# QKV products of a decoder's self-attention as a 2x2 block product in seven products, with heads in pairs

## The chip, the cores and the metric

The kernel runs on one core of a Trainium2 chip. Its engines are TensorE (PE, matmuls; PEld is its weight load), VectorE (DVE), ScalarE (ACT), GpSimd (POOL) and SyncE (SP, which issues most transfers). The metric is the device time of one launch in microseconds; lower is better.

## The reference

A decoder of two layers over 16 sequences of 112 tokens, 1024 wide, in float32. The change touches the self-attention of the second layer, where "sequence" runs over the first axis of `x`, of length 16 (`sbh` with s = 16, b = 112), so attention is causal over 16 positions, for 112 independent columns:

```python
def _L1_attn_ref(tokens, weight_qkv, weight_proj):
    NUM_HEADS, NUM_KV_HEADS, HEAD_DIM = (32, 8, 128)
    Q_PER_GROUP = NUM_HEADS // NUM_KV_HEADS
    qkv = jnp.einsum('sbh,ph->sbp', tokens, weight_qkv)
    qkv = qkv.reshape(S, B, NUM_KV_HEADS, Q_PER_GROUP + 2, HEAD_DIM)
    ...
    scores = jnp.einsum('bhsd,bhtd->bhst', q, k) * scale
    scores = jnp.where(causal, scores, jnp.finfo(scores.dtype).min)
    attn = jax.nn.softmax(scores, axis=-1)
    out = jnp.einsum('bhst,bhtd->bhsd', attn, v)
    return jnp.einsum('sbe,he->sbh', out, weight_proj)

x = _layernorm(x + _L1_attn_ref(x, L1_attn_weight_qkv, L1_attn_weight_proj), axis=-1)
```

So 1792 tokens are multiplied with 6144 x 1024 weights (8 groups of one key, one value and four query units of 128 features), 32 heads attend, and 4096 x 1024 weights project back.

## The kernel before

Three stages run one after the other: `token_stage` for layer 0, `self_attention` for layer 1, `token_stage` for the rest of layer 1. Only `self_attention` differs (and where the experts' weights lie in a shared buffer).

The 1792 tokens are handled in two halves of 896 (`TH`; seven chunks `c` of 128 tokens, `NC`). Each half runs over the eight key/value heads; one half and one head is a group `G`, so there are 16 groups. Every product of float32 data is three products of rounded parts, hi x hi, hi x lo, lo x hi (`split_passes`, type float32r). The tokens, transposed, lie in `x_hi` and `x_lo` for the half at hand; the rows of the second half are prepared one per group in groups 0 to 6 (`early`), stored, and reloaded at group 8 (`NKV`).

A group on TensorE: units K, V, Q0 to Q3. A unit is `product` (L1445) twice, over 480 and 416 columns (K, V) or 480 and 360 (Q: the first of the 16 positions needs no query, its columns lie last), each with 8 k-tiles x 3 passes accumulated in one PSUM bank. Inside the units come the transposes of the values (`turn_values`, L1474), the scores of a head (`scores`, L1466, one burst of 28 small matmuls, 56 records) and, after the next group's K, the weighing (`weigh`, L1487: four matmuls of 32 rows for each chunk) and the projection (`project`, L1504: for each chunk and each half of the output 4 heads x 3 passes of 512 columns). Projections go through a ring of three PSUM banks; each key of the table `slot` says which.

GpSimd walks down a table `splits`: for each 128 x 1024 piece of weights it waits for the load and for a free buffer, casts it to the hi part (L1386) and subtracts to get the lo part (L1388). `w_hi`/`w_lo` hold two units, `p_hi`/`p_lo` the four heads' projection weights. SP loads pieces in the same order through two buffers `raw`. ScalarE copies products from PSUM to `qT`, `kT`, `vT` (L1589), takes exponentials (L1598) and casts the weighed values (L1612). VectorE does the softmax (L1711 to L1728), the low parts of the weighed values (L1733) and adds the projection to `acc` (L1745). At a half's end the group's last scores, weighing and projection follow with no next group to hide them (`ends_half`).

Every order is written out by hand; nothing is scheduled by a planner.

## Time and profile before

| | us |
|---|---|
| median of 3 runs | 3245.8 (3244.6 to 3246.4) |
| span of the profiled execution | 3248.6 |
| TensorE busy | 3091.6 (95%) |
| VectorE busy | 1803.7 (56%) |
| ScalarE busy | 1341.0 (41%) |
| GpSimd busy | 873.5 (27%) |
| self-attention, first product to last projection | 830.2 to about 2546 |

Busy times are those of one profiled execution, counted from its first instruction. Matmuls are pipelined, so the record of one is longer than the distance to the next; where the pace matters, one reads the starts. The granted clock of TensorE is 1.00 at 2.4 GHz and 0.50 at 1.2 GHz. Lines named L... are those of the kernel before; in the section on the order of the changed kernel they are those of the changed one.

### The profile page before, as it was taken

Reading aid. Unit: us, or ns where it says so; the run is one execution under the profiler, and the core shown is the slowest. Engines: PE = TensorE matmul, PEld = TensorE weight load, DVE = VectorE, ACT = ScalarE, POOL = GpSimd, SP = SyncE. Lnnn points to the kernel's source line nnn. Section 1 sums busy time; section 2 is a strip of 40 time slices with the busy share of each in tenths; the row PEclk is TensorE's granted clock in tenths of the full one; section 3 lists DMA queues with packets and bytes.
Section 4 is the critical chain, followed back from the end, with each engine's and each line's share of the span. In section 5 each row is a group of like instructions: output and inputs, shape, how many; then the busy total and the mean of one; then the engine's idle time right before and its main releaser. Section 6 shows DMA issues by size and latency. Waiting matters only on the chain. (4 is left out here: it accounts for less than half of the span.)

```text
span 3248.6 us, 67042 instructions
## 1 busy us (share of the span) xinstructions
PE 3091.6 (95%) x25912; PEld 2575.3 (79%) x25912; DVE 1803.7 (56%) x4632; ACT 1341.0 (41%) x3692; POOL 873.5 (27%) x751
## 2 busy tenths in 40 slices
PE   5999999996999999999989999999999699999997
PEld 3888888874788888888878888888887578888886
DVE  6788888885424332544253323333243488888885
ACT  2777877774211111111111111111111487777774
POOL 3222222211423432243225332443233011111110
PEclk8999999996899999999999999999999899999999
DMA  9777777752212311231144111221124656555551
GB/s 282 187 188 188 195 199 189 188 144 91 72 52 79 92 58 53 72 92 59 52 163 143 53 59 60 84 76 55 53 72 156 161 148 151 151 151 151 151 148 44
DMA packets 226622, 386.73 MB, mean 119 GB/s; under 512 B 55953, under 2 KB 177137, under 8 KB 225794
## 3 DMA queue, kind: packets, MB, share of 16 engines
q1 hardware_dynamic: 222848, 380.25, 42.2%
q8 instruction: 207, 3.39, 0.5%
q10 hardware_dynamic: 3458, 2.20, 0.2%
q14 instruction: 109, 0.89, 0.1%
HBM read 291.46 MB, written 90.91 MB: 118 GB/s over the span
## 5 line engine op out<-in xcount | busy, mean ns | idle before, releaser
L749 ACT ACTIVATE L_probs<-L_masked,L_least 112x375 f32<-112x375 f32 x1024 | 627.8, 615 | 80.0 <-DVE L_least L878 75.7
L878 DVE CUSTOM_DVE_ANT_0 L_masked<-L_scores,L_nmask 112x375 f32<-112x375 f32 x1024 | 552.6, 544 | 174.3 <-PE L_scores L482 137.0
L1445 PE MATMUL sa_banks<-both_hi,sa_w_hi 128*128 128x480 f32 (+2 forms) x1536 | 560.2, 365 | 2.0 <-DVE both_lo L1704 2.0
L1445 PE MATMUL sa_banks<-both_lo,sa_w_hi 128*128 128x480 f32 (+2 forms) x1536 | 550.6, 358 | 0.0
L1445 PE MATMUL sa_banks<-both_hi,sa_w_lo 128*128 128x480 f32 (+2 forms) x1536 | 549.7, 358 | 0.0
L487 PEld LDWEIGHTS L_turned<-ident_sb,L_probs 112*125 112x125 f32 x3072 | 457.1, 189 | 108.2 <-issue 48.2
L487 PE MATMUL L_turned<-ident_sb,L_probs 112*125 112x112 f32 x3072 | 526.7, 280 | 7.6 <-ACT L_probsT L744 3.9
L482 PE MATMUL L_scores<-L_krep,L_qrep 128*112 128x376 f32 x1024 | 418.1, 409 | 7.8 <-DMA L_qrep<-query_parts 6.0
L744 ACT COPY L_probsT<-L_turned 125x336 f32<-125x336 f32 x768 | 337.3, 439 | 177.8 <-PE L_turned L487 170.6
L1745 DVE TENSOR_TENSOR sa_acc<-sa_acc,sa_banks 128x512 f32<-128x512 f32 x224 | 154.1, 688 | 416.9 <-PE sa_banks L1504 416.9
L1504 PE MATMUL sa_banks<-sa_p_hi,sa_o_hi 128*128 128x512 f32 x896 | 365.5, 408 | 0.0
L1504 PE MATMUL sa_banks<-sa_p_lo,sa_o_hi 128*128 128x512 f32 x896 | 355.3, 397 | 0.0
L1504 PE MATMUL sa_banks<-sa_p_hi,sa_o_lo 128*128 128x512 f32 x896 | 355.0, 396 | 0.0
L1445 PEld LDWEIGHTS sa_banks<-both_hi,sa_w_hi 128*128 128x128 f32 x1536 | 288.9, 188 | 34.7 <-issue 6.8
L1711 DVE SCALAR_TENSOR_TENSOR sa_sm<-sa_banks,sa_causal 128x224 f32<-128x224 f32 x64 | 25.1, 392 | 511.0 <-PE sa_banks L1466 511.0
L1445 PEld LDWEIGHTS sa_banks<-both_hi,sa_w_lo 128*128 128x128 f32 x1536 | 288.9, 188 | 23.5
L1445 PEld LDWEIGHTS sa_banks<-both_lo,sa_w_hi 128*128 128x128 f32 x1536 | 289.4, 188 | 21.7
L1612 ACT CAST sa_o_hi<-sa_banks 128x512 fp32r<-128x512 f32 x112 | 66.0, 589 | 508.4 <-PE sa_banks L1487 506.7
L384 POOL TENSOR_TENSOR L_attn<-L_attn,L_xcur 112x512 f32<-112x512 f32 x64 | 82.6, 1291 | 588.5 <-DVEq L891 588.5
L1388 POOL TENSOR_TENSOR sa_w_lo<-sa_raw,sa_w_hi 128x1024 fp32r<-128x1024 f32 x96 | 230.0, 2396 | 14.4 <-issue 1.0
L1386 POOL CAST sa_p_hi<-sa_raw 128x1024 fp32r<-128x1024 f32 x64 | 66.6, 1041 | 565.6 <-PE sa_banks L1504 554.4
L1504 PEld LDWEIGHTS sa_banks<-sa_p_hi,sa_o_hi 128*128 128x128 f32 x896 | 169.0, 189 | 47.9 <-issue 0.4
(289 smaller groups left out, 5055.3 us busy)
## 6 DMA issues: line engine op xcount, KB each, us to landing
L_qrep<-query_parts SPq DMA_DIRECT2D x256, 224.0 KB, 6.2
sa_raw<-in_wqkvU_dram SPq DMA_DIRECT2D x96, 512.0 KB, 3.5
L_krep<-ctx_parts SPq DMA_DIRECT2D x256, 188.0 KB, 4.2
sa_raw<-in_wprojU_dram SPq DMA_DIRECT2D x64, 512.0 KB, 3.5
query_parts<-L_qT_hi SPq DMA_DIRECT2D x64, 224.0 KB, 8.4
query_parts<-L_qT_lo SPq DMA_DIRECT2D x64, 224.0 KB, 9.3
L_xcur<-x SPq DMA_DIRECT2D x32, 448.0 KB, 5.1
L_val<-in_ctx_dram SPq DMA_DIRECT2D x64, 187.5 KB
```

What stands on the lines that cost most here:

```text
L384: p.tensor_tensor(attn[0:S, cols], attn[0:S, cols], xcur[0:S, cols], ALU.add).then_inc(sum_ok, 1)
L482: pe.matmul(scores[0:S, (NH * t + n) % 3, 0:TP], qrep[:, gq, r, gi, :], krep[:, 4 * gq + gi, :], start=True, stop=True).then_inc(score_ok, 1)
L487: mm = pe.transpose(turned[0:TC, m % 2, S * j:S * j + S], probs[0:S, m % 4, TC * j:TC * j + TC], ident[0:S, 0:S])
L744: nc.scalar.copy(probsT[:, m % 8, :, :], turned[0:TC, m % 2, 0:TJ * S].rearrange("p (j s) -> p j s", s=S)).then_inc(copied_s, 1)
L749: nc.scalar.activation(probs[0:S, e % 4, :], masked[0:S, e % 4, :], ACT.Exp, bias=least[0:S, e:e + 1], scale=-1.0, accum_out=rsum[0:S, e:e ...
L878: v.tensor_tensor_reduce(out=masked[0:S, n % 4, :], in0=scores[0:S, (NH * t + n) % 3, 0:T], in1=nmask[0:S, :], scale=1.0, scalar=HUGE, op0 ...
L1386: nc.gpsimd.tensor_copy(hi, src)
L1388: done = nc.gpsimd.tensor_tensor(lo, src, hi.bitcast(F32), ALU.subtract)
L1445: mm = pe.matmul(feat[u % 2][i][:, 0:t.stop - t.start], a[:, u % 2, k, :], b[:, k, t], start=(n == 0), stop=(n == 3 * KT - 1))
L1504: mm = pe.matmul(out, a[:, j, c % 2, :], b[:, j, 512 * h:512 * h + 512], start=(i == 0), stop=(i == 3 * QPG - 1))
L1612: nc.scalar.copy(o_hi[:, :, c % 2, :].rearrange("p j (b t) -> p j b t", b=4), mixed).then_inc(o_hi_ok, 1)
L1745: v.tensor_tensor(acc[:, c, cols], acc[:, c, cols], ring[:, b, :], ALU.add).then_inc(ring_free[b], 1)
```

## The change

Two units are now one block product. With the weights of a pair of units as a 2 x 2 matrix (unit by half of the 1024 inputs) and the tokens as a 2 x 2 matrix (half of the inputs by half of the columns of a half), seven products of blocks replace eight: `B11, T1, T2, B21, T3, T4, B22`. The pairs are (K, V), (Q0, Q1), (Q2, Q3), named `KV`, `Q01`, `Q23`. Each product is 4 k-tiles x 3 passes of 448 columns (`KV`) or 420 (queries).

- The token operands (seven blocks, three of them quarters of the transposed rows and four differences) are made by VectorE once per row (`differences`, `low_parts`) and ScalarE (`copy_turned`, `high_parts`), and lie in a larger `x_hi`, `x_lo`.
- The weight operands are made anew for every pair by GpSimd (`weights`): besides cast and subtraction, one sum each for T1 and T2 and two for T3, each 512 columns wide, into a ring of four operands (`RING`). Operand `n` waits for product `n - 4`. The ring lies in one memory region in the first half and in the other in the second; the projection's weights of a pair of heads lie in the remaining one (`heads`).
- Products accumulate in four banks; ScalarE keeps three intermediate sums per pair (`keep`), VectorE adds four times per pair (`combine`) and writes the features.
- Heads go in pairs: one softmax for two heads, two projections per group with two heads each, so twice as many weighings (64 columns) and twice as many additions to `acc`. The pair Q01's scores, one group's second pair of heads and so on are placed by hand: the second pair of heads of group G - 1 is projected between Q01 and Q23 of group G, the first pair of G after Q23.
- The rows of the second half are prepared in groups 1 to 7 and not 0 to 6 (`late_row`), in two rounds through one buffer.
- SP loads half pieces of 512 columns through six buffers.

The core of the diff, GpSimd and TensorE:

```diff
-                nc.gpsimd.tensor_copy(hi, src)
-                pool.drain()
-                done = nc.gpsimd.tensor_tensor(lo, src, hi.bitcast(F32), ALU.subtract)
...
+            def weights(G, pr, start=0, stop=OPS):
...
+                source = (a11, mid[:], mid[:], a12, a11, a22, a12)
+                for o in range(start, stop):
+                    n = OPS * (3 * G + pr) + o
+                    if n >= RING:
+                        pool.wait_ge(prod_ok, n - RING + 1)
...
+                    if o == T1:
+                        loaded(first + 2)
+                        p.tensor_tensor(mid[:], a21, a22, ALU.add)
+                    if o == T2:
+                        pool.drain()
+                        p.tensor_tensor(mid[:], mid[:], a11, ALU.subtract)
+                    if o == T3:
+                        pool.drain()
+                        p.tensor_tensor(a11, a11, a21, ALU.subtract)
+                        p.tensor_tensor(a12, a12, mid[:], ALU.subtract)
...
+                weights(G, Q01)
+                if late_project(G):
+                    heads(G - 1, 1)
+                weights(G, Q23)
+                heads(G, 0)
...
+                for o in range(OPS):
+                    first_weighted = late_project(G) and o == B22
+                    product(G, Q01, o, (lambda: weigh(G - 1, 1, 0)) if first_weighted else None)
+                    if r is not None and o == B11:
+                        turn_row(1, r, late)
+                if late_project(G):
+                    project(G - 1, 1)
...
+                combine(G, Q01, 2)
+                combine(G, Q01, 3)
+                if late_project(G):
+                    accumulate(G - 1, 1)
```

GpSimd, before, in the second half: the rows of half a group (`w` a unit, `p` a head, each row with the semaphores that it waits for; `feat_ok` comes from TensorE).

```order
L1386 CAST sa_p_hi<-sa_raw 128x1024 [waits sa_proj_ok,sa_ld_raw1]
L1388 TENSOR_TENSOR sa_p_lo<-sa_raw,sa_p_hi 128x1024
L1386 CAST sa_w_hi<-sa_raw 128x1024 [waits sa_feat_ok,sa_ld_raw0]
L1388 TENSOR_TENSOR sa_w_lo<-sa_raw,sa_w_hi 128x1024
L1386 CAST sa_p_hi<-sa_raw 128x1024 [waits sa_ld_raw1]
L1388 TENSOR_TENSOR sa_p_lo<-sa_raw,sa_p_hi 128x1024
```

Units and heads alternate there, and a unit is two instructions of 1024 columns. After, in the second half, from the fifth operand of Q01 to the projection's weights behind it (`r1` is the ring of operands, `r0` the heads' weights, `mid` the running sum):

```order
L1452 TENSOR_TENSOR sa_raw<-sa_raw 128x512 [waits sa_prod_ok]
L1453 TENSOR_TENSOR sa_raw<-sa_raw,sa_mid 128x512
L1428 CAST sa_r1_hi<-sa_raw 128x512
L1430 TENSOR_TENSOR sa_r1_lo<-sa_raw,sa_r1_hi 128x512
L1428 CAST sa_r1_hi<-sa_raw 128x512 [waits sa_prod_ok]
L1430 TENSOR_TENSOR sa_r1_lo<-sa_raw,sa_r1_hi 128x512
...
L1428 CAST sa_r0_hi<-sa_raw 128x1024 [waits sa_ld_raw0,sa_proj_ok]
L1430 TENSOR_TENSOR sa_r0_lo<-sa_raw,sa_r0_hi 128x1024
L1428 CAST sa_r0_hi<-sa_raw 128x1024 [waits sa_ld_raw1]
L1430 TENSOR_TENSOR sa_r0_lo<-sa_raw,sa_r0_hi 128x1024
```

The heads' weights now stand in one piece behind all seven operands of Q01, each of which waits for a product.

VectorE, before, at the start of a projection: the softmax's last rows, then the low parts (`o_lo`), then the additions.

```order
L1724 TENSOR_TENSOR sa_ex<-sa_ex,sa_total 128x224
L1728 STREAM_TRANSPOSE sa_probsT<-sa_ex 32x7x32 x4
L1733 TENSOR_TENSOR sa_o_lo<-sa_banks,sa_o_hi 128x4x128 [waits sa_o_hi_ok] x2
L1745 TENSOR_TENSOR sa_acc<-sa_acc,sa_banks 128x512 [waits sa_proj_ok] x2
L1733 TENSOR_TENSOR sa_o_lo<-sa_banks,sa_o_hi 128x4x128 [waits sa_o_hi_ok]
```

After, at the start of the projection behind Q23:

```order
L1885 TENSOR_TENSOR sa_smex<-sa_smex,sa_total 128x448
L1889 STREAM_TRANSPOSE sa_probsT<-sa_smex 32x448 x4
L1865 TENSOR_TENSOR sa_qT<-sa_banks,sa_kept 128x7x15x4 [waits sa_kept_ok,sa_prod_ok] x4
L1895 TENSOR_TENSOR sa_o_lo<-sa_banks,sa_o_hi 128x2x128 [waits sa_o_hi_ok] x2
L1910 TENSOR_TENSOR sa_acc<-sa_acc,sa_banks 128x512 [waits sa_proj_ok] x2
```

Between the softmax and the first low part now stand the four combinations, the last of which waits for the pair's last product.

## Rows read from the trace of the kernel before

**Rows 1.** Windows (columns: stretch, length, busy by engine with instructions, granted clock, DMA share, GB/s).

```profile
1900.00:2000.00 100.00, 99.72 (x720) 84.73 (x719) 32.24 (x59) 12.53 (x26) 37.90 (x22) 1.00 0.22 69
```

**Rows 2.** Timeline of TensorE across a projection and the next products (start us, duration us, engine, line).

```profile
1793.03 0.39 PE L1504 MATMUL sa_banks<-sa_p_lo,sa_o_hi 128*128 128x512 f32 x1
...
1798.16 0.39 PE L1504 MATMUL sa_banks<-sa_p_hi,sa_o_lo 128*128 128x512 f32 x1
...
1816.43 0.38 PE L1445 MATMUL sa_banks<-both_hi,sa_w_hi 128*128 128x480 f32 x1
...
1821.65 0.35 PE L1445 MATMUL sa_banks<-both_hi,sa_w_hi 128*128 128x416 f32 x1
...
1826.14 0.38 PE L1445 MATMUL sa_banks<-both_hi,sa_w_hi 128*128 128x480 f32 x1
...
1832.11 0.33 PE L1445 MATMUL sa_banks<-both_hi,sa_w_hi 128*128 128x360 f32 x1
...
1834.45 0.33 PE L1445 MATMUL sa_banks<-both_hi,sa_w_lo 128*128 128x360 f32 x1
```

**Rows 3.** Timeline of TensorE: last matmul before a weighing; around a score burst.

```profile
1791.94 0.39 PE L1504 MATMUL sa_banks<-sa_p_hi,sa_o_lo 128*128 128x512 f32 x1
...
882.64 0.37 PE L1445 MATMUL sa_banks<-both_hi,sa_w_lo 128*128 128x480 f32 x1
...
882.94 0.70 PE L1466 MATMUL sa_banks<-sa_kT,sa_qT 128*32 128x32 f32 x56
883.57 0.48 PE L1445 MATMUL sa_banks<-both_hi,sa_w_hi 128*128 128x480 f32 x1
883.89 0.38 PE L1445 MATMUL sa_banks<-both_lo,sa_w_hi 128*128 128x480 f32 x1
```

**Rows 4.** GpSimd by line and form (count | busy us, mean ns | idle before).

```profile
L1388 POOL TENSOR_TENSOR sa_w_lo<-sa_raw,sa_w_hi 128x1024 fp32r<-128x1024 f32 x96 | 230.0, 2396 | 14.4 <-issue 1.0
...
L1386 POOL CAST sa_w_hi<-sa_raw 128x1024 fp32r<-128x1024 f32 x96 | 99.9, 1041 | 388.0 <-PE sa_banks L1445 369.2 <-DMA sa_raw<-in_wqkvU_dram 18.3 <-issue 0.5
...
L395 POOL TENSOR_TENSOR L_wq_lo<-L_oT,L_wq_hi 128x512 fp32r<-128x512 f32 x1 | 1.3, 1287 | 0.1
...
L393 POOL CAST L_wq_hi<-L_oT 128x512 fp32r<-128x512 f32 x1 | 0.6, 619 | 0.0
```

**Rows 5.** Timeline of GpSimd inside a group, three instructions in a row.

```profile
1837.60 2.40 POOL L1388 TENSOR_TENSOR sa_w_lo<-sa_raw,sa_w_hi 128x1024 fp32r<-128x1024 f32 x1
1840.17 1.04 POOL L1386 CAST sa_p_hi<-sa_raw 128x1024 fp32r<-128x1024 f32 x1 [0.18 <-issue]
1841.36 2.42 POOL L1388 TENSOR_TENSOR sa_p_lo<-sa_raw,sa_p_hi 128x1024 fp32r<-128x1024 f32 x1
```

**Rows 6.** VectorE: the probabilities' product twice (timeline), and additions by line.

```profile
1841.45 2.57 DVE L1724 TENSOR_TENSOR sa_ex<-sa_ex,sa_total 128x224 f32<-128x224 f32 x1
...
1861.51 0.39 DVE L1724 TENSOR_TENSOR sa_ex<-sa_ex,sa_total 128x224 f32<-128x224 f32 x1
...
L1745 DVE TENSOR_TENSOR sa_acc<-sa_acc,sa_banks 128x512 f32<-128x512 f32 x224 | 154.1, 688 | 416.9 <-PE sa_banks L1504 416.9
```

**Rows 7.** TensorE: end of a half, after a short wait (timeline); clock (windows).

```profile
1655.25 0.81 PE L1487 MATMUL sa_banks<-sa_probsT,sa_val 32*128 32x128 f32 x8 [6.04 <-DVEq L1729]
...
848.06 0.46 PE L1445 MATMUL sa_banks<-both_hi,sa_w_hi 128*128 128x416 f32 x1 [2.01 <-DVE both_lo L1704]
...
850.00:860.00 10.00, 10.00 (x46) 9.58 (x45) 0.00 (x0) 1.14 (x4) 4.91 (x4) 0.86 0.07 11
```

**Rows 8.** First product and first query product (TensorE); VectorE's work on one row.

```profile
830.21 0.77 PE L1445 MATMUL sa_banks<-both_hi,sa_w_hi 128*128 128x480 f32 x1
...
858.95 0.38 PE L1445 MATMUL sa_banks<-both_hi,sa_w_hi 128*128 128x480 f32 x1
...
L1683 DVE SCALAR_TENSOR_TENSOR sa_acc<-sa_banks,sa_gate,sa_acc 128x512 f32<-128x512 f32 x14 | 10.3, 744 | 7.2 <-PE sa_banks L1417 7.2
...
806.37 1.29 DVE L1689 BATCH_NORM_STATS2 sa_st<-sa_acc 128x6 f32<-128x512 f32 x2
```

**Rows 9.** DMA issues of the page (KB each, us to landing).

```profile
sa_raw<-in_wqkvU_dram SPq DMA_DIRECT2D x96, 512.0 KB, 3.5
```

More of the change, by code:

```diff
@@ L1240, in self_attention @@
         EARLY0, EARLY1, STORE0, STORE1 = (NC * i for i in range(4))
+        made = lambda half, c, i: OPS * NC * half + OPS * c + sum(len(x) for x in ROUNDS[:i])
+        heads_done = lambda G, hp: 2 * NC * (nth[G, hp] + 1)
         @block.sync
@@ L1450, in unit @@
-            def unit(G, u, between, later={}):
-                pe.wait_ge(unit_ok, UNITS * G + u + 1)
-                def landed():
-                    pe.wait_ge(feat_sb, UNITS * G + u)
-                    between()
-                product(G, u, 0, {3: landed})
-                product(G, u, 1, later)
-            def scores(G, j):
-                if QPG * G + j:
-                    pe.wait_ge(score_free, QPG * G + j)
-                for c in range(NC):
-                    for p in range(4):
-                        t = slice(P * c + 32 * p, P * c + 32 * p + 32)
-                        mm = pe.matmul(score[32 * p:32 * p + 32, 32 * c:32 * c + 32], qT[:, j, t], kT[:, G % 2, t],
-                                       start=True, stop=True)
+                    out = bank("turn", c, h) if half else banks[:, 2 * (c % 2) + h, :]
@@ new lines, in scores @@
+            def scores(G, hp):
+                m = 3 * G + Q01 + hp
+                pe.wait_ge(comb_ok, 4 * m + 4)
+                if 2 * G + hp:
+                    pe.wait_ge(score_free, 2 * G + hp)
+                for j in range(2):
+                    for c in range(NC):
+                        for q in range(4):
+                            at = NV * (q // 2) + CK * c + 32 * (q % 2)
+                            mm = pe.matmul(score[32 * q:32 * q + 32, 32 * (NC * j + c):32 * (NC * j + c) + 32],
+                                           qT[:, j, at:at + 32], kT[:, at:at + 32], start=True, stop=True)
@@ L1506, in project @@
                                 i += 1
                         mm.then_inc(proj_ok, 1)
+                    if c == 0 and after_first:
+                        after_first()
             pe.wait_ge(log_ok, 1)
[L1510 removed]
+            pe.matmul(banks[:, 3, 0:1], ones, lsum[:], start=True, stop=True).then_inc(mean_ok, 1)
             pe.wait_ge(ld_z, 16)
```

882 lines of the change are left out of this document (512 added, 370 removed).

## Prediction

> **What bounds the kernel now.** I read the windows first, then TensorE's timeline inside one group of heads, then the groups by line for GpSimd and VectorE. In a steady 100 us of self-attention TensorE is busy 99.7 us at full granted clock, VectorE 32, ScalarE 13, GpSimd 38 [rows 1]. So this stage lasts as long as the matmuls that TensorE is given, plus what it must wait for. Its true pace is the distance between starts: 24 steps of 480 columns take 5.22 us (0.218 each), 24 of 416 take 4.49 (0.187), 14 of 360 take 2.34 (0.167), 22 of 512 take 5.13 (0.233) [rows 2]. GpSimd, with 38 us of 100, is hidden today; the reader should watch it, because the change gives it most of the new work.
>
> **The matmuls: -121 us.** A group (16 of them) has now 2 units of 24 x (480 + 416) and 4 of 24 x (480 + 360) columns: 2 x 9.71 + 4 x 9.23 = 56.3 us. After: three block products of 7 x 12 matmuls, 448 wide (K, V) and 420 wide (Q). No row has these widths; between the rows for 416 and 480 they come to 0.202 and 0.189 us: 84 x 0.202 + 168 x 0.189 = 48.8. Saved 7.55 per group, 121 in all. The bound on the other side is the 480 row for every matmul (x is now read in seven pieces of 60 or 64 columns, which no row shows): that gives back up to 98.
>
> **The smaller pieces on TensorE: +47.** Heads in pairs double the weighing steps from 7 to 14 per group and halve their width to 64. One step of 128 columns costs 0.62 us: two starts of the projection lie 1.09 apart across it, less two steps of 0.233 [rows 2, 3]. If all of the 0.43 that is not the plain switch of a score burst (below, 0.19) shrank with the width it would be 0.41; if it is bound by loading 128 weight columns, which stays, 0.62. I take 0.55, nearer to the row as it is: 14 x 0.55 - 7 x 0.62 = +3.3 per group, +53 (+22 to +69). Score matmuls are as many as before but come in two bursts rather than four: a burst of 56 costs 1.25 - 2 x 0.218 = 0.81, of which 0.63 lies between its start and that of the next product, so 0.19 is switch [rows 3]; a burst of 112 is 1.4, and two of these for four of those save 0.4 per group, -6. Projections have the same 168 matmuls.
>
> **GpSimd: +110.** Its durations: 2.40 us for a subtraction of 1024 columns and 1.04 for the cast; of 512 columns, 1.29 and 0.62 [rows 4]. Gaps between them are 0.15 and 0.18 [rows 5]. An operand of 512 costs 0.62 + 0.15 + 1.29 + 0.18 = 2.24; T1 adds one sum (3.6), T2 one (3.7), T3 two (5.0). A pair is 4 x 2.24 + 12.3 = 21.3 us; TensorE multiplies it in 17.0 (K, V) or 15.9 (Q). Before, a pair cost 2 x 3.8. Over a group this is 3 x 21.3 + 4 x 3.8 = 79 of some 105, so the sum alone doesn't bind; the order does. Operand n needs product n - 4 done, so GpSimd enters K,V with four operands ready and starts the fifth when the first product is done, at 2.9. From there it must do 3 operands of K,V (9.5), 7 of Q01 (21.3) and then both projection splits (7.5), which stand behind Q01: ready at 41.2. TensorE would want them at 17.0 + 1.4 (scores) + 15.9 + 0.6 (weighing) + 1.25 (next part) = 36.2. It waits 5.1, part of it at T3 of Q01 (about 1.8), the rest before the projection; with the 1.25 that it would lose anyway 6.3, in 14 groups: 88. Groups 0 and 8 have no projection between Q01 and Q23: 59.6 us of GpSimd's work from 2.9 against 51.7 of TensorE's gives 10.8 each: 22. For Q23 it has the whole projection before it (24 us) to make four operands, and is in time.
>
> The page GPSIMD Engine Reference of the Trainium skill (3.1, Elementwise) gives about 2.6 cycles an element at 1.2 GHz for tensor_tensor; by that 512 columns would take 1.11 us, the wait would shrink by 3.3 per group and the sum by 46. The row says 1.29, and the row is used.
>
> **The start of a projection: +15.** After the last product of a pair VectorE must first combine it, then make the low part of the first weighed chunk, and only then TensorE goes on: 0.43 from the last start to the end, 0.6 for the combination and 0.4 for the low part (448 and 256 columns, between 0.39 at 224 and 0.69 at 512 [rows 6]), less the usual 0.2: 1.25. Twice a group; beside GpSimd's wait it is inside the 6.3; alone it stands in 12 groups.
>
> **Groups 1 to 7: +24.** The row of the second half that is prepared there now goes in two rounds through one buffer; round two of ScalarE waits until eight stores of round one have landed, VectorE's low parts wait for that, and the combination that the first weighing needs is queued behind them. With T3's operand made 12 us into Q01, eight issues and then a landing of the kind of a weight load (3.5 [rows 9]; about as much for the issues, an estimate) the projection begins about 2 us after GpSimd would allow, and GpSimd has 1.3 of roots more: 3.4 x 7.
>
> **The ends of the halves: -7.** Now TensorE idles 6.0 in one piece there [rows 7], with two smaller gaps around it and a lower clock after: about 9 each. After, the first pair's probabilities are ready when Q23 ends (2.6 of chain), but the second pair's softmax is threaded through VectorE's accumulations and holds two ring banks (3): 5.6 each.
>
> **The prologue: +22.** Today products begin at 830.2, with four of seven rows ready, and K and V are done at 859.0 [rows 8]. After, the first product needs all seven. VectorE's part of a row is 3.1 as now (0.74 x 2, 1.3 for the statistics, 0.2 [rows 8]) plus 11 subtractions of 256 columns at about 0.42: 7.7; with the hand-overs to ScalarE (a norm, two copies and seven casts a row) 9.5. From 801 this gives 855 to 864; I take 862, plus 17 and 2 of low clock: 881 against 859.
>
> **Clock: +10.** After the idle 2.0 at 848 the granted clock of the next 10 us is 0.86 [rows 7]. A wait of 5 in each group should cost about 0.7 again, 0 to 1.4.
>
> VectorE's other additions are hidden: accumulations double to 28 x 0.69 [rows 6] and 12 combinations come in, some 53 us of 105 in all, and softmax (7 us at 448 columns) ends before T3 does. DMA moves the same weights.
>
> **Sum.** -121 + 47 + 110 + 15 + 24 - 7 + 22 + 10 = +100 on the profiled 3248.6, whose span lies 3 above the median of the runs, 3245.8: 3346.
>
> **Rivals.** (1) GpSimd keeps up: its waits fall to the 1.25 of the chain (-90), the stores hide (-14), no clock loss (-10): 3232, faster. It decides at a pair of 18.8 us or less, 12% under what the rows give; for it speaks only that GpSimd's total is under TensorE's. 8%. (2) VectorE holds GpSimd up. A VectorE product of 224 columns with both inputs in SBUF took 2.57 us when it began just after a GpSimd subtraction (at 1841.36) and 0.39 when it didn't [rows 5, 6]: the two exclude each other. If GpSimd in turn waits for such operations (two of 0.63 in K,V and Q01), its chain grows by 1.3 a group, 18 in all, and with deeper clock dips (+10) the time is 3374. 20%. The SBUF — State Buffer page of the Trainium skill (two separate sides) says so: whichever starts first has the port for the whole instruction, and the other blocks. The row shows one of the two directions; no row shows GpSimd held. (3) The half-wide weighing costs 0.41: 3315. 15%. (4) The products don't come at 7/8 of the time, since the pieced reading slows them to the pace of 480 columns: +98, 3444. 5%. My forecast 3346: 50%. The last 2% lie about no change.
>
> **Numbers.** The range is to hold 8 times in 10: the low end takes half of rival 3, half the prologue and no clock or store loss (3285), and some of the way to rival 1: 3265. The high end is rival 2 with the dear weighing: 3400. A measurement of this kernel tells 0.2% (6.5 us) from no change. Faster 7% (rival 1), same 3% (rival 1 at the least of its gain, and the 2%), slower 90%.
>
> **What would show it.** Right: GpSimd over 70% busy in the stage, TensorE idle some 5 us once per group before the projection that follows Q01, put down to GpSimd's low part; product starts 0.20 and 0.19 apart; first product near 862. Wrong: if TensorE stays at 99% in a steady 100 us, GpSimd's chain is overrated; if GpSimd's 512-column subtraction is not 1.29 or the steps overlap, the 110 falls; if the product starts lie 0.218 apart, the 121 does.

## The result, and the profile after

The changed kernel takes 3439.9 us (median of 4 runs, 3433.1 to 3445.5) against 3245.2 (4 runs): a ratio of 1.060, 95% interval 1.058 to 1.061. It was forecast slower, at 3346; it is slower by twice as much. The profiled execution spans 3443.7 us, 195.1 more than the one before.

The windows of the profile after show both halves of the stage (columns as in [rows 1]): 1100 to 1200 lies in the first half, where rows are prepared beside the heads, 2000 to 2100 in the second.

```profile
1100.00:1200.00 100.00, 85.53 (x546) 72.87 (x545) 50.13 (x66) 16.25 (x32) 63.17 (x58) 0.90 0.25 82
2000.00:2100.00 100.00, 93.12 (x712) 79.15 (x710) 42.94 (x66) 10.90 (x24) 72.82 (x64) 0.97 0.21 69
```

Where [rows 1] has TensorE at 99.7 of 100 us and a granted clock of 1.00, it is now idle for 7 to 14 us, and the clock has fallen too. GpSimd has 73 us of work in the second half, as forecast. Who is waited for stands in the waits of TensorE from 800 to 2760 (waiting line, releaser, us in total, times, longest; L1577 is a product, L1612 a weighing, L1865 VectorE's combination, L1895 a low part of weighed values, L1430 GpSimd's low part of weights):

```profile
PE sa_banks L1612 <- DVE sa_qT L1865: 49.1, 9, 7.3
PE sa_banks L1612 <- POOL sa_r_lo L1430: 38.9, 9, 4.3
PE sa_banks L1577 <- POOL sa_r_lo L1430: 34.4, 21, 4.1
PE sa_banks L1612 <- DVE sa_o_lo L1895: 29.4, 24, 1.3
PE sa_banks L1577 <- DVE both_lo L1849: 11.8, 1, 11.8
```

In the second half each group looks like this on TensorE, from the fifth product of Q01 to the projection behind it:

```profile
2184.74 0.46 PE L1577 MATMUL sa_banks<-both_hi,sa_r_hi 128*128 128x420 f32 x1 [1.27 <-POOL sa_r_lo L1430]
2185.03 0.35 PE L1577 MATMUL sa_banks<-both_lo,sa_r_hi 128*128 128x420 f32 x1
...
2189.07 0.35 PE L1577 MATMUL sa_banks<-both_lo,sa_r_hi 128*128 128x420 f32 x1
...
2196.84 0.70 PE L1612 MATMUL sa_banks<-sa_probsT,sa_val 32*128 32x64 f32 x8 [4.32 <-POOL sa_r_lo L1430]
2197.47 0.80 PE L1631 MATMUL sa_banks<-sa_r_hi,sa_o_hi 128*128 128x512 f32 x1
2198.06 0.63 PE L1631 MATMUL sa_banks<-sa_r_lo,sa_o_hi 128*128 128x512 f32 x1
2198.49 0.63 PE L1631 MATMUL sa_banks<-sa_r_hi,sa_o_lo 128*128 128x512 f32 x1
...
2205.37 0.40 PE L1631 MATMUL sa_banks<-sa_r_hi,sa_o_lo 128*128 128x512 f32 x1
2205.69 0.45 PE L1612 MATMUL sa_banks<-sa_probsT,sa_val 32*128 32x64 f32 x8
2206.07 0.50 PE L1631 MATMUL sa_banks<-sa_r_hi,sa_o_hi 128*128 128x512 f32 x1
2206.41 0.39 PE L1631 MATMUL sa_banks<-sa_r_lo,sa_o_hi 128*128 128x512 f32 x1
```

The two waits for GpSimd stand where the prediction put them, at T3 (1.3) and before the projection (4.3). 21 steps of 420 columns take 4.04 us, 0.192 each (2185.03 to 2189.07), so the product does come at about 7/8 of the time. Across a weighing two starts lie 1.04 apart (2205.37 to 2206.41), less two steps 0.57. What was not forecast in this size is the third thing: behind the wait the 512-column matmuls start 0.43 apart instead of 0.23.

In the first half the wait is another. Around the same place in group 3, first SyncE (SPq: the first of eight stores) and ScalarE, then GpSimd, VectorE and TensorE:

```profile
1248.41 0.43 SPq L1342 DMA_DIRECT2D xt_hi<-both_hi  x1
...
1253.97 1.15 ACT L1708 CAST both_hi<-sa_late 128x256 fp32r<-128x256 f32 x2 [3.28 <-DMA xt_lo<-both_lo]
1255.03 0.61 ACT L1708 CAST both_hi<-sa_dif 128x256 fp32r<-128x256 f32 x1
```

```profile
1257.23 2.38 POOL L1430 TENSOR_TENSOR sa_r_lo<-sa_raw,sa_r_hi 128x1024 fp32r<-128x1024 f32 x1
1257.38 2.61 DVE L1849 TENSOR_TENSOR both_lo<-sa_dif,both_hi 128x256 fp32r<-128x256 f32 x1
1259.91 0.85 DVE L1865 TENSOR_TENSOR sa_qT<-sa_banks,sa_kept 128x420 f32<-128x420 f32 x1
...
1260.91 0.70 PE L1612 MATMUL sa_banks<-sa_probsT,sa_val 32*128 32x64 f32 x8 [7.34 <-DVE sa_qT L1865]
```

ScalarE's second round waits for the eight stores of the first; VectorE's low parts follow, and the last of them takes 2.61 us: GpSimd began a subtraction 0.15 earlier, and the low part ends 0.4 after it (the run with casts below tests this). The combination stands behind it, and TensorE waits 7.3 for that. GpSimd had the heads' weights at 1259.6, so it is not what this wait ends with; without VectorE's queue it would be late itself, as a run below shows.

### The profile page after: what moved, and what is told of

The parts are those of the page before. It is cut to its first block and busy times, and to the rows that moved or that the text cites. A ratio compares the mean times of both kernels' runs of the same rounds, so it can differ in the third digit from the quotient of the medians.

```text
span 3443.7 us, 70284 instructions
## 1 busy us (share of the span) xinstructions
PE 3101.1 (90%) x26232; PEld 2571.2 (75%) x26232; DVE 2116.8 (61%) x4937; ACT 1378.1 (40%) x3762; POOL 1436.0 (42%) x1423
## 5 line engine op out<-in xcount | busy, mean ns | idle before, releaser
L1577 PE MATMUL sa_banks<-both_hi,sa_r_hi 128*128 128x420 f32 (+1 forms) x1344 | 500.2, 372 | 47.1 <-POOL sa_r_lo L1430 34.4
L488 PEld LDWEIGHTS L_turned<-ident_sb,L_probs 112*125 112x125 f32 x3072 | 458.2, 190 | 107.6 <-issue 48.0
L1577 PE MATMUL sa_banks<-both_lo,sa_r_hi 128*128 128x420 f32 (+1 forms) x1344 | 490.2, 365 | 0.0
L1577 PE MATMUL sa_banks<-both_hi,sa_r_lo 128*128 128x420 f32 (+1 forms) x1344 | 489.5, 364 | 0.0
L1430 POOL TENSOR_TENSOR sa_r_lo<-sa_raw,sa_r_hi 128x512 fp32r<-128x512 f32 (+1 forms) x304 | 466.8, 1536 | 45.2 <-issue 2.3
L1631 PE MATMUL sa_banks<-sa_r_hi,sa_o_hi 128*128 128x512 f32 x896 | 393.2, 439 | 7.6 <-DVE sa_acc L1910 7.6
L1631 PE MATMUL sa_banks<-sa_r_lo,sa_o_hi 128*128 128x512 f32 x896 | 368.5, 411 | 0.0
L1631 PE MATMUL sa_banks<-sa_r_hi,sa_o_lo 128*128 128x512 f32 x896 | 368.3, 411 | 0.0
L1577 PEld LDWEIGHTS sa_banks<-both_hi,sa_r_hi 128*128 128x128 f32 x1344 | 257.2, 191 | 79.7 <-POOL sa_r_lo L1430 42.3
L1577 PEld LDWEIGHTS sa_banks<-both_lo,sa_r_hi 128*128 128x128 f32 x1344 | 257.9, 192 | 13.2
L1577 PEld LDWEIGHTS sa_banks<-both_hi,sa_r_lo 128*128 128x128 f32 x1344 | 257.8, 192 | 12.6
L1865 DVE TENSOR_TENSOR sa_qT<-sa_banks,sa_kept 128x420 f32<-128x420 f32 x128 | 114.4, 894 | 243.9 <-PE sa_banks L1577 164.4
```

Of the source, the lines that this page charges most:

```text
L488: mm = pe.transpose(turned[0:TC, m % 2, S * j:S * j + S], probs[0:S, m % 4, TC * j:TC * j + TC], ident[0:S, 0:S])
L1430: p.tensor_tensor(lo, src, hi.bitcast(F32), ALU.subtract).then_inc(done, 1)
L1577: mm = pe.matmul(out_of[o][:, 0:width], a[:, n % RING, k, :], right, start=(o in opens and i == 0), stop=(i == 3 * HALF_KT - 1), skip_grou ...
L1631: mm = pe.matmul(out, a[:, j, n % 2, :], b[:, j, 512 * h:512 * h + 512], start=(i == 0), stop=(i == 5))
L1865: v.tensor_tensor(dst, src, held, ALU.add).then_inc(comb_ok, 1)
```

## Where the 195 us are

I took the span apart at the end of the first K,V pair (before 858.95, after 898.81). Idle times of 0.3 and more on TensorE's timeline are summed; the clock's share is TensorE's busy time in windows of 2 us times one less the granted clock of the window; the work is the rest.

| | predicted | measured |
|---|---|---|
| prologue, to the end of the first K,V pair | +22 | +40 |
| TensorE's work | -121 + 47 = -74 | -59 |
| waits | 110 + 15 + 24 - 7 = +142 | 159.8 - 15.0 = +145 |
| clock | +10 | 74.0 - 4.9 = +69 |
| sum | +100 | +195 |

So the miss is the clock (59), the prologue (18), the work (15) and 3 of waits. That the waits agree in sum is partly luck. By groups they are, forecast and measured: groups 0 and 8 together 21.6 and 17.4, groups 1 to 6 65.7 and 71.5, groups 9 to 14 45.3 and 40.6, the ends of the halves 7 less than before and 0.5 less. The experiments ask whether this reading holds.

## Experiments

**GpSimd's lateness.** The first leaves out its four sums per pair:

```diff
-                        p.tensor_tensor(mid[:], a21, a22, ALU.add)
...
-                        p.tensor_tensor(mid[:], mid[:], a11, ALU.subtract)
...
-                        p.tensor_tensor(a11, a11, a21, ALU.subtract)
-                        p.tensor_tensor(a12, a12, mid[:], ALU.subtract)
```

> The changed kernel without GpSimd's four sums per pair (the operands of T1, T2 and T3 are then plain pieces of the weights, so products of other numbers are added up; the work of every other engine is as before the edit). In its own profile the changed kernel takes 110.2 us for a group of the second half and 118.4 to 120.5 for one of groups 1 to 6. Theory (GpSimd's order binds the second half, VectorE's queue behind the row's second round binds the first): a pair costs GpSimd 15.6 instead of 21.3, so its waits of 1.3 and 4.3 go, with the 2 of low clock behind them, and a group of the second half takes about 102.5; groups 0 and 8 lose 10 each; groups 1 to 7 keep their wait of 5.8 to 7.3 at the weighing, which ends with VectorE's combination, and gain 2 at most: about 3353. Rival (GpSimd's lateness binds both halves): groups 1 to 7 fall by 8 as well: about 3310.

Measured 3327.3, between the two. The second half is as the theory says (102.6 to 102.8 in groups 10 to 13, no wait for GpSimd). Groups 1 to 6 fell to about 113 (group 2: 119.6), 6.4 on average, nearer to the rival's 8 than to the 2 that I gave them, and the longest wait left there is one of 3.4 for VectorE's combination. Groups 9 and 14 took 104.3 and 105.9 with the same two waits of 1.3 as their neighbours: the granted clock fell at one and at both of these, which cost 1.5 and 3.2 (TensorE's busy time times one less the clock, as in the table above).

The second keeps all work and gives the ring six operands in the second half:

```diff
+        def depth(n):
+            return RING if n < FIRST6 + RING else 6
```

> The changed kernel with six weight operands in the ring instead of four, in the second half only (the two more lie where the rows' operands were staged in the first half). GpSimd's work is the same, it may only run further ahead while TensorE projects, when it stands still for 10.6 us. Theory (the order and the short ring make GpSimd late, not its total of 79 us per group): groups 9 to 15 fall from 110.2 to about 102.5, group 8 by about 8, the first half stays: about 3378. Rival (the loads of raw weights hold GpSimd up once it may run ahead, since six buffers of 512 columns are all it has): half of that at most, about 3410.

Measured 3383.0. Groups 9 to 14 take 102.2 to 102.4, at a granted clock of 1.00, with 70 us of GpSimd's work in 100 where it had 73: not its total but its order and short ring made it late. The loads don't hold it up.

The third gives two casts a group to ScalarE:

```diff
+            def cast_heads(G, j):
...
+                nc.scalar.copy(heads_of(G, 1)[0][:, j, :], raw[:, i % 6:i % 6 + 2, :].rearrange("p x n -> p (x n)")).then_inc(cast_ok, 1)
```

> The changed kernel with ScalarE casting the high parts of the heads' weights that stand between Q01 and Q23 (two casts of 1024 columns a group); GpSimd only subtracts. That takes 2.4 us from GpSimd's chain in 14 groups. Theory (GpSimd binds the second half alone): the wait of 4.3 before the projection falls to 1.9 in groups 9 to 15, with a part of the low clock behind it, 20 in all, nothing in groups 1 to 7: about 3420. Rival (it binds in both halves, or the casts on ScalarE come too late and hold the pair's kept sums up): 3400, or 3440 and more.

Measured 3404.7, 35 under the changed kernel where the theory gave 20. The first half, where it gave nothing, took 10 less in groups 1 to 7, so GpSimd counts there too, as the rival had it. The wait of 4.3 became 2.1 in groups 9 to 14, and these take 104.8 to 108.2: 104.8 and 104.9 are the groups in which the granted clock stayed at 1.00, the others lost 1.7 to 3.4 to it. Halving a wait took away its clock loss in some groups, not in all.

**The rows of the second half.** One run leaves them out of groups 1 to 7:

```diff
-    late_row = lambda G: G - 1 if 1 <= G <= NC else None
+    late_row = lambda G: None
```

> The changed kernel without the preparation of the second half's rows in groups 1 to 7 (no gated sum, norm, transposes, differences, high and low parts, stores and reloads; the second half multiplies the first half's tokens again). Theory (this preparation costs the first half all that its groups take more than those of the second): groups 1 to 6 fall from 120 to about 110, group 7 by 9 too, together about 70: 3370. The prediction's own step for it (2.6 of TensorE's work and 3.4 of waiting): 6 each, 42 together: 3398. What is over 2.6 per group is price of the waits and of the clock behind them.

Measured 3365.6. Without rows the first half's groups take 110, as the second half's (group 2 again 7 more): a row costs 9.3 where the prediction's step, with the 2.6 of TensorE's own work on a row, had 6.

The next only moves VectorE's low parts of the second round behind the combinations:

```diff
                 combine(G, Q01, 1)
-                if r is not None:
-                    low_parts(1, r, 1)
...
+                    if row is not None and 1 <= c <= 3:
+                        low_parts(1, row, 1, c - 1)
```

> The changed kernel with one thing moved: in groups 1 to 7 VectorE makes the three low parts of the row's second round not ahead of Q01's last two combinations but one at a time between the additions of the projection that follows, and their stores are issued one place later. Theory (the weighing inside Q01's last product waits 5.8 to 7.3 because the combination it needs is queued behind these low parts, which wait for eight stores to land): that wait goes, and what is late next is GpSimd, which had the heads' weights 24.5 us after Q01's start where TensorE went on at 30.8: 5.6 us and some clock less in each of seven groups, about 40 in all: 3400. Rivals: the low parts now delay the additions that free the three PSUM banks, 2 us a group: 3414; or the weighed values' cast on ScalarE is itself behind the second round's casts, which wait for the same stores: nothing gained, 3437.

Measured 3393.0. The wait for the combination is gone from all seven groups. Groups 1 and 3 to 6 take 113.6 to 114.8 (group 2: 119.6), and GpSimd is late next (2.8 to 4.4 before the projection). The queue behind the stores was the cause in the first half.

Then GpSimd's subtractions become casts:

```diff
-                p.tensor_tensor(lo, src, hi.bitcast(F32), ALU.subtract).then_inc(done, 1)
+                p.tensor_copy(lo, src).then_inc(done, 1)
```

> The changed kernel with the low part of every weight operand made by a second cast instead of a subtraction (so it is no low part, and the products' sums are wrong; every other engine's work is unchanged). This shortens GpSimd's chain by some 12 us per group, so GpSimd is never late; and it takes away the two-input instructions on which GpSimd and VectorE exclude each other, all but the four sums of a pair. Theory with the lock (VectorE's 256-column low parts of 1.4 to 2.8 us in groups 1 to 7, against 0.59 in the prologue, are held by GpSimd's subtractions): VectorE's queue is some 5 us shorter there, the waits of 5.8 to 7.3 mostly go, and beside the second half's 63 and group 0's 10 another 50 are saved: about 3318. Without the lock (those parts are slow by their own form) groups 1 to 7 stay near 118: about 3355.

Measured 3318.3. VectorE's low parts by line and form from 1000 to 1700, of the changed kernel first, then of this one:

```profile
L1849 DVE TENSOR_TENSOR both_lo<-sa_dif,both_hi 128x256 fp32r<-128x256 f32 x17 | 28.3, 1686 | 0.0
L1849 DVE TENSOR_TENSOR both_lo<-sa_late,both_hi 128x256 fp32r<-128x256 f32 x17 | 23.9, 1434 | 14.8 <-ACT both_hi L1708 14.3
```

```profile
L1849 DVE TENSOR_TENSOR both_lo<-sa_dif,both_hi 128x256 fp32r<-128x256 f32 x18 | 14.7, 842 | 0.0
L1849 DVE TENSOR_TENSOR both_lo<-sa_late,both_hi 128x256 fp32r<-128x256 f32 x18 | 12.5, 717 | 14.6 <-ACT both_hi L1708 14.0
```

They halve although nothing about them was changed: GpSimd's two-input instructions hold VectorE's. The changed kernel's own timeline from 760 on says the same. A low part that stands alone in it takes 0.58 to 0.62 us when GpSimd is idle at its start (9 of them), 1.46 to 1.55 when a two-input instruction of 512 columns is under way there (14), and 2.61 under one of 1024 columns (7). The combination, which reads one input from PSUM and one from SBUF, is hardly touched: 0.92 on average under a two-input instruction, 0.87 with GpSimd idle (137 and 21). The other direction, the prediction's rival 2, is hardly seen: GpSimd's 512-column subtraction of raw weights takes 1313 ns on average after, 1287 in [rows 4]. The page SBUF — State Buffer of the Trainium skill (two separate sides) says that whoever starts first has the port. The rows above agree with it in one direction, which the trace of before had shown too [rows 5, 6], and for which I had priced nothing; I had priced only the other.

**The prologue.** First another order of the rows' steps (VectorE's part; ScalarE casts a row ahead of norming the next but one):

```diff
+                if c >= 2:
+                    differences(0, c - 2)
                 gated_sum(0, c, acc[:, c, :])
                 moments(EARLY0 + c, acc[:, c, :])
                 if c >= 2:
-                    differences(0, c - 2)
                     low_parts(0, c - 2)
```

> The changed kernel with another order in the prologue: VectorE makes the statistics of row c + 2 between the differences and the low parts of row c, and ScalarE casts row c's high parts ahead of norming row c + 2. Theory (rows go round in a circle of 11.3 us: statistics, root, norm, copy, seven casts of 0.62 and seven low parts of 0.59, one after the other, where VectorE's own work is 8.8): the circle falls to about 9, five times: the first product some 12 earlier, 3427. Rival (ScalarE and VectorE are simply slower in this layout, nothing is won by order): 3440.

Measured 3427.4: the first product at 866.8 (872 to 879 in the runs with the prologue unchanged). Counted from VectorE's first gated sum, which itself comes at 797 to 804, the first product comes after 68.2 us where the runs with the prologue unchanged have 74.4 to 75.6. So the order gives 7 of the 12 expected, and a row goes round in 9.8; the other 5 or so of the total were not followed up. Then the plain layout:

```diff
-            return src.rearrange("p k (l b) -> p k b l", b=LEN)
+            return src
```

> The changed kernel with the tokens' operands and the combinations written in plain order, not with the 16 positions turned outward in pieces of four (so the columns no longer belong together as attention needs; same counts and sizes). Theory (the small pieces make these operations dear): a 256-column cast on ScalarE falls from 0.62 to about 0.37, a low part on VectorE from 0.59 to 0.42, a combination from 0.90 to 0.60, as the prediction had them; the rows of the prologue go round in 9 instead of 11.3 and the start of each projection is 0.3 shorter: 3415. Rival (these are the prices of their sizes): durations and time as they were, 3440.

Measured 3413.6, the first product at 863.3, 65.6 after the first gated sum. Two groups by line and form, of the changed kernel first, and VectorE's low parts in the prologue (800 to 885, and 800 to 870):

```profile
L1865 DVE TENSOR_TENSOR sa_qT<-sa_banks,sa_kept 128x420 f32<-128x420 f32 x128 | 114.4, 894 | 243.9 <-PE sa_banks L1577 164.4 <-ACT sa_kept L1724 76.5 <-issue 3.0
L1708 ACT CAST both_hi<-sa_kept 128x256 fp32r<-128x256 f32 x12 | 6.7, 624 | 0.0
L1849 DVE TENSOR_TENSOR both_lo<-sa_kept,both_hi 128x256 fp32r<-128x256 f32 x12 | 6.5, 591 | 0.0
```

```profile
L1864 DVE TENSOR_TENSOR sa_qT<-sa_banks,sa_kept 128x420 f32<-128x420 f32 x128 | 76.0, 594 | 280.1 <-PE sa_banks L1577 182.8 <-ACT sa_kept L1724 94.4 <-issue 3.0
L1708 ACT CAST both_hi<-sa_kept 128x256 fp32r<-128x256 f32 x12 | 4.2, 401 | 0.7 <-DVE sa_kept L1835 0.5
L1849 DVE TENSOR_TENSOR both_lo<-sa_kept,both_hi 128x256 fp32r<-128x256 f32 x12 | 4.4, 419 | 0.0
```

The prediction's 0.6 and 0.42 are right for rows read and written in one piece. Turned in pieces of four, the same sizes cost 0.89 and 0.59.

**The clock.** The kernel before, with pauses of several lengths:

```diff
+                    if c == 1 and G in PAUSE:
...
+                        for _ in range(PAUSE[G]):
+                            nc.scalar.copy(late[:, 0:512], late[:, 512:1024])
+                            act.drain()
```

> The kernel before, with nothing but pauses added: in groups 8 to 14 ScalarE makes 9, 11, 12, 13, 15, 17 and 21 idle copies of 512 columns between two chunks of the projection, so that TensorE waits once per group, each time longer (none to some 6 us; the trace says how long). A group takes 104.4 there without them. Theory (the prediction's missing 95 us are mostly the clock: after a wait TensorE goes on at 1.2 GHz for a while): a wait of up to about 1 costs itself, one of 4 and more costs itself and 2 to 4 on top, with matmuls of 512 columns 0.43 instead of 0.23 apart behind it. Rival (the prediction's 0.7 per wait holds, and the loss in the changed kernel has another cause): itself and 0.7.

Measured 3292.4. The waits, and the periods of groups 9 to 14, in which the first six lie (104.4 without them); for the last wait, in group 15, the period is 104.4 and the 12.0 that the stretch around it takes longer than before:

| wait | 2.1 | 3.2 | 3.8 | 4.5 | 5.9 | 7.2 | 10.3 |
|---|---|---|---|---|---|---|---|
| period | 106.6 | 109.2 | 109.9 | 111.7 | 112.8 | 113.5 | 116.4 |
| more than the wait | 0.1 | 1.6 | 1.7 | 2.8 | 2.5 | 1.9 | 1.7 |

Behind the wait of 4.5, TensorE's timeline:

```profile
2102.47 0.81 PE L1488 MATMUL sa_banks<-sa_probsT,sa_val 32*128 32x128 f32 x8 [4.52 <-DVE sa_o_lo L1739]
...
2104.23 0.63 PE L1505 MATMUL sa_banks<-sa_p_hi,sa_o_lo 128*128 128x512 f32 x1
2104.66 0.63 PE L1505 MATMUL sa_banks<-sa_p_hi,sa_o_hi 128*128 128x512 f32 x1
```

A single wait costs itself, and the six of 3.2 to 10.3 us another 1.6 to 2.8 each, in a kernel that is otherwise the one before. The extra does not grow with the wait. The size is nearer to the theory than to 0.7, at or under the low end of the 2 to 4 I gave.

In the changed kernel itself, the waits are filled:

```diff
+            def idle_matmuls(G, hp, count):
+                out = bank("proj", G, hp, 0, 0)
+                for i in range(count):
+                    pe.matmul(out[:, 0:320], x_hi[:, 0, 0, 0:P], x_hi[:, 0:2, 0, 0:160], start=True, stop=True)
```

> The changed kernel, exact, with matmuls that nobody needs laid into its longest waits: in groups 1 to 7 30 of 320 columns ahead of the weighing inside Q01's last product (some 4.5 us of the 5.8 to 7.3 that TensorE waits there), in groups 9 to 15 26 of them ahead of the projection behind Q01 (3.9 of 4.3). They go to the bank that the projection then overwrites. Theory (each long wait costs, beside itself, a stretch at 1.2 GHz behind it, 3.7 us a group in the second half and about 6 in the first): the clock stays at 1.00 there, the releasers come when they came before, and the time falls by some 3 per group, 40 in all: 3400; the profile shows 512-column matmuls 0.23 apart right behind the wait. Rival (the added work comes on top, or the clock falls all the same): 3440 to 3500.

Measured 3420.5 (3415.5 to 3427.3), half of the theory's gain. In the second half, the filling and what follows:

```profile
2179.49 3.95 PE L1620 MATMUL sa_banks<-both_hi 128*128 128x320 f32 x26
2184.04 0.45 PE L1613 MATMUL sa_banks<-sa_probsT,sa_val 32*128 32x64 f32 x8 [0.60 <-POOL sa_r_lo L1431]
2184.42 0.50 PE L1639 MATMUL sa_banks<-sa_r_hi,sa_o_hi 128*128 128x512 f32 x1
2184.76 0.39 PE L1639 MATMUL sa_banks<-sa_r_lo,sa_o_hi 128*128 128x512 f32 x1
2184.99 0.39 PE L1639 MATMUL sa_banks<-sa_r_hi,sa_o_lo 128*128 128x512 f32 x1
```

The releaser comes as late as before, the matmuls behind it are 0.23 apart, and groups 10 to 14 take 107.0 to 107.5 instead of 109.7 to 111.0. There work that nobody needs, laid into a wait, gave back some 3 us a group; that is the clock, as a cause and not only as a reading. In the first half groups stayed at 119.5: the clock falls there all the same, at 1362, 1376 and 1424 of group 4, behind the waits that were left (2.4 at T3, the unfilled 1.5 of the long one and 1.3 soon after it, 1.3 behind Q23). So for the first half no filling shows the clock's price; there it rests on the granted clock in the windows, and on the runs with shorter waits: groups 1 to 6 lose 5.1 to 7.7 with waits of 10.4 to 14.5 in all, and 0 to 1.7 with 4.3 to 5.6 in the last but one run below.

**Group 2** is 5 to 7 us longer than its neighbours:

```diff
                 if G == NKV:
+                    for one in stale:
+                        pool.sem_clear(one)
...
-                if G == 2:
-                    for one in stale:
-                        pool.sem_clear(one)
```

> The changed kernel with GpSimd's clearing of the first stage's semaphores moved from group 2 to the end of the first half, where GpSimd stands idle. Theory (group 2 takes 125.3 against 118.4 to 120.5 of its neighbours, with one more wait of 4.1 for GpSimd at the start of Q01, because this clearing, which was hidden while GpSimd had 62 us of 100 free, is now in its chain): group 2 falls to 119, 6 less: 3434. Rival (another cause in group 2): it stays at 125.

Measured 3429.4, and group 2 takes 120.2 like the others. The clearing takes GpSimd 6.8 us ("issue" in its timeline). The kernel before has it in group 2 too, where GpSimd had 62 us of 100 free [rows 1]. My step list passed it over.

**All together.** The next five build on each other; the edits of the first are those shown above.

> Four of the edits together, all of them exact: the ring of six in the second half, the row's second low parts threaded through the additions, the prologue's order, and the heads' casts on ScalarE. Theory (their losses lie in different places, but the last comes to count in the first half only now that VectorE's queue is out of the way): 3440 - 57 - 47 - 13 - 20 = about 3303; groups 1 to 7 near 111, groups 9 to 15 near 102.4. Rival (they overlap, the gain of the row's order is GpSimd's gain): 3320 and more.

Measured 3316.6. Groups 9 to 14 take 102.2 to 102.6, groups 3 to 6 110.4 to 112.6, as expected; in all it is 13 over the 3303 that the gains added up to, nearer to the rival's 3320, which I did not trace further.

```diff
+                cast_operand(G, KV, T4)
                 keep(G, KV, 2)
+                cast_operand(G, Q01, B11)
...
+                cast_operand(G, Q01, B21)
                 keep(G, Q01, 0)
```

> The kernel of the four edits, with four more of GpSimd's casts per group on ScalarE: the high parts of T4 of the K, V pair and of B11, B21 and T4 of Q01, each 0.61 and a gap. Theory (in the first half, with a ring of four, GpSimd is late by its chain from the K, V pair's fifth operand to the heads' weights, 41 us after the group's start where TensorE wants them at 36): this takes 3.1 more from it, so the wait before the projection all but goes: groups 1 to 7 at about 107, groups 0 and 8 some 6 less each: about 3262. Rival (ScalarE's casts stand behind its kept sums and hold GpSimd up in turn): 3300, as without it.

Measured 3321.2, a miss by 59. The first half came to 108.3 in groups 4 to 6 (the theory had 107), but the second half rose to 104.4 and more: there GpSimd had been in time, and now waited for ScalarE.

```diff
                 combine(G, Q01, 2)
+                if late_project(G):
+                    low_weighted(G - 1, 1, 0)
                 combine(G, Q01, 3)
```

> The kernel before this one, with VectorE making the low part of the first weighed chunk ahead of the pair's last combination and not behind it, twice a group. Theory (the wait of 1.3 at the start of each projection is VectorE's combination of 0.9 and this low part of 0.4 one after the other, and the chunk was weighed inside the last product): some 0.9 less at 28 places, 25 in all: about 3237, level with the kernel before (3245) or a little under it. Rival (the next chunk's weighing needs the combination's bank or the cast on ScalarE, so the wait stays): 3262.

Measured 3314.2 (3305.9 to 3318.9), 7 less than the one before where 25 were expected; the theory's 3237 had also built on the gain that the run before did not bring. In the second half the wait of 1.3 behind Q23 is gone, which gives 1.2 a group; behind Q01 TensorE waits 1.4 for the casts moved to ScalarE and for GpSimd behind them, with the low part ready or not. In the first half a wait of 1.0 for GpSimd took the place of the one behind Q23.

```diff
-    late_cast = lambda G, hp: hp == 1 and not ends_half(G)
+    late_cast = lambda G, hp: hp == 1 and G < NKV - 1
...
-                    weights(G, KV, 0, RING)
+                    weights(G, KV, 0, 6)
```

> The kernel of the last run of the former set, with ScalarE's casts of operands and heads' weights in the first half only (in the second the ring of six had made GpSimd timely, and the casts on ScalarE held it up: 104.4 a group against 102.3), all six operands ready before the second half, and the clearing of semaphores moved to the end of the first half. Theory: 1.5 to 2 less in each group of the second half, 5 at group 8, 6 at group 2: 3314 - 13 - 5 - 6 = about 3290, still over the kernel before (3245), because the prologue (27), TensorE's waits of 3 to 4 a group in the first half and the smaller pieces remain. Rival: the first low part ahead of the last combination lets the second half fall below 101: 3280 or less.

Measured 3279.8 (3276.4 to 3281.7), 1.011 of before (1.009 to 1.012), as the rival had it. A window of its second half:

```profile
2050.00:2150.00 100.00, 99.80 (x766) 85.20 (x765) 49.61 (x76) 12.02 (x27) 72.92 (x65) 1.00 0.21 69
```

Groups 9 to 14 take 99.7 to 99.9 with no wait of 0.3 or more, where the kernel before takes 104.4; the prediction's terms for TensorE alone give 104.3 - 7.55 + 3.3 - 0.4 = 99.7.

```diff
-            by_act.append((G, KV, T4))
+            by_act += [(G, KV, T3), (G, KV, T4), (G, KV, B22)]
```

> The version before it, exact, with GpSimd relieved once more in the first half: ScalarE also casts T3 and B22 of K, V and of Q01 and the heads' weights of the first pair; in the second half the clearing of semaphores goes to group 11 and the last four row roots stand behind the fifth and sixth operand (in the version before, all seven stood behind them, and TensorE waited 7.5 at the end of the first half). Theory (the 4.3 us that groups 1 to 6 still wait are GpSimd's, three places of 1 to 1.6, and the clock holds once they are short): groups 1 to 6 from 108.5 to about 106, group 0 about 5 less, group 7 about 9 less: 3280 - 15 - 5 - 9 = about 3250, level with the kernel before (3245). Rival (ScalarE is now the one that is late, its casts stand behind the row's copies and casts): groups 1 to 7 stay at 108.5: 3266.

Measured 3280.5 (3272.4 to 3283.5): nothing gained over the one before, where 30 were expected. TensorE's waits for GpSimd fell to 0.4 in groups 1 to 6, but at 107.1 to 108.0 they are hardly shorter: TensorE now waits 2.3 to 2.6 in Q01's last product for a combination that is queued behind the row's first low parts, which GpSimd's subtractions hold up (0.59 by themselves, 1.6 there). And clearing in group 11 made that group 107.8 beside 100.2. No version here beats the kernel before. In the last but one (which also waits 7.5 at the end of the first half, where the row roots stood behind the six operands) the first K,V pair ends at 885.3 against 858.95: 26 of its 29 us of span over before (the medians are 35 apart) are the prologue, and behind it what the block product saves (4.6 a group in the second half) about pays for the first half and the ends.

## Why the prediction was wrong, point by point

- **Products (-121).** Right: 0.192 for 420 columns against the 0.189 taken, and the pieced reading (rival 4) did not slow them. That rival's 3444 is near the measured 3440 by chance; its mechanism did not come about.
- **Smaller pieces (+47).** Right: 0.57 a weighing against 0.55. Both together are shown by the 99.8 of a group without waits. The measured work of the whole stage is 15 higher than forecast. In groups 9 to 14 of the changed kernel it is 100.1 to 100.6 where 99.7 was forecast, in groups 1 to 6 102.8 to 103.0 where 106.9 before and the same saving make 102.3: some 7 in these twelve groups. The rest lies in groups 0, 7, 8 and 15. I did not follow it up.
- **GpSimd (+110).** Right in the second half: place, releaser and size (1.3 and 4.3, 5.6 of the 6.3 with the chain). The runs with sums left out and with a longer ring show the mechanism. Groups 0 and 8 waited 7.6 and 9.8 where 10.8 each was forecast. Rival 2, GpSimd held up by VectorE, did not come about: its instructions grew by 2%.
- **Start of a projection (+15).** Right in size (1.3 against 1.25), though not in its parts: the combination takes 0.89 and not 0.6.
- **Rows in groups 1 to 7 (+24).** The place and the queue were right, and the stores landed in 5.6 us rather than 7. The low parts have no price of their own in this step (0.42 each in the prologue's), and they take 1.5 to 2.6 beside a subtraction of GpSimd. The wait for GpSimd hides under this one, so the waits of a group come to 10.4 to 12.1 (14.5 in group 2) where 10.9 was forecast.
- **Ends of the halves (-7).** Not gained: beside the usual waits of groups 7 and 15 TensorE waits 6.6 and 7.9 there, against 8.1 and 6.9 before; four of these waits (0.8 to 3.1) are for additions that free ring banks.
- **Prologue (+22, measured +40).** The step that failed is "with the hand-overs to ScalarE (a norm, two copies and seven casts a row) 9.5": a row takes 11.4, since casts (0.62) and low parts (0.59) cost more in this layout and the two engines' steps for a row follow each other. Some 5 of the 18 belong to this one execution.
- **Clock (+10, measured +69).** The step that failed is the price of a wait: "a wait of 5 in each group should cost about 0.7 again". It was read from one window of 10 us behind one wait of 2.0 [rows 7], and only half of what that window gives: 10 us of busy TensorE at 0.86 have lost 1.4. Nor had the shorter waits of a group (at T3, at the start of a projection) a price in clock. By the 2 us windows the groups lost 2.7 to 4.3 in the second half and 5.1 to 7.7 in groups 1 to 6; a single wait of 4.5 us cost 2.8 in the run with pauses. That is 59 of the 95 us.

By the rule in the page GPSIMD Engine Reference of the Trainium skill (3.1, Elementwise) the forecast would have been 46 less, and further off. The trace does not agree with the estimate of 1.11 us worked out from it: GpSimd's 512-column subtraction takes 1.29 to 1.31 after, 1.29 before.

## What to carry to other kernels

A wait of TensorE, where TensorE bounds the kernel, has two prices, its length and the time at the lower clock behind it. For the single waits of 3.2 to 10.3 us here the second was a sixth to two thirds of the first. It was met behind waits of 1.3 too, in some groups and not in others with the same waits, so one long wait a period should be priced with it from the start, and short ones with a range. When work is moved to a helper engine, its total says little: ask how far ahead its ring lets it run, what else stands in its queue (here a clearing of semaphores and the other engine's held instructions), and whether the moved instruction is priced in the layout that it will really have.

## What I had not expected of the hardware

- The granted clock fell to 0.50 while TensorE waited and stayed there 9 us into the work that followed, through further short waits. The 7.3 of group 3 (columns as in [rows 1]):

```profile
1254.00:1256.00 2.00, 0.00 (x0) 0.00 (x0) 1.37 (x1) 1.65 (x3) 1.86 (x1) 1.00 0.00 0
1256.00:1260.00 4.00, 0.00 (x0) 0.00 (x0) 4.00 (x4) 0.00 (x0) 3.43 (x2) 0.52 0.00 0
1260.00:1264.00 4.00, 3.09 (x14) 2.37 (x14) 0.76 (x1) 0.37 (x1) 0.00 (x0) 0.50 0.61 198
1264.00:1268.00 4.00, 2.70 (x14) 2.23 (x14) 1.54 (x3) 0.37 (x1) 0.61 (x1) 0.50 0.93 265
1268.00:1272.00 4.00, 4.00 (x21) 2.97 (x20) 1.78 (x3) 0.37 (x1) 3.61 (x4) 0.78 0.68 260
```

- With ScalarE casting the heads' weights, waits of the same length (0.9 and 2.1, in groups 9 to 13) were followed by the lower clock in three groups (107.6, 108.2, 107.6) and not in the two others (104.9, 104.8). Without GpSimd's sums, two waits of 1.3, 45 us apart, were followed by it in group 9 (one of the two) and group 14 (both), and not in groups 10 to 13.
- A low part of 256 columns on VectorE took 2.61 us when it began during a GpSimd subtraction of 1024 columns, 0.59 alone; GpSimd's instructions grew by 2%.
- Pieces of four columns made a 256-column cast on ScalarE 0.62 instead of 0.40 and a 420-column addition on VectorE 0.89 instead of 0.59.
